# A fused decoder layer: the risk branch outside the batch loop, steering before the last places, and the experts' gate and up product turned

## The chip, the cores and the metric

One Trainium2 chip, one core. The metric is device time of one execution in microseconds (us), here the median of three executions. The engines are TensorE (PE; its weight loads are PEld), VectorE (DVE), ScalarE (ACT), GpSimd (POOL) and SyncE (SP), which only issues transfers.

## What is computed

A decoder layer in fp32 on x of shape (4, 512, 256), with three residual parts, each on a layer norm of x:

```
x = x + self_attention(norm(x))          # causal, 16 heads of 64, bias by distance
x = x + cross_attention(norm(x), ctx)    # 16 heads of 16, 1601 keys a batch, RMS norm of q and k
x = x + experts(norm(x))                 # 32 experts and 8 "zero" experts, top 6 of 40 a token
scores = softmax(h @ classifier.T); top 6 of scores + bias; weight = 2.5 * score
y_e = (silu(h @ Wgate_e.T) * (h @ Wup_e.T)) @ Wdown_e.T      # intermediate width 128
out = h * (sum of weights of zero experts) + sum_e weight_e * y_e
```

## The kernel before, in words

The program has three parts in one block; each engine runs its part of all three one after the other, without a barrier.

**Self attention** (`self_attention`) is not touched.

**Cross attention** (`cross_attention`). A batch is 52 slots (4 groups of 4 heads by 13 tiles of keys). In slot s of batch b PE computes the scores of four heads for one tile of keys (`scores`, line 1226), the product with V of two slots earlier (`times_v`, line 1241), and one step of a written plan (`prepare`): a step of the next batch's keys and queries, or "o" (turning finished heads). ACT takes the exponential of the scores (line 1385, two a slot) and is the engine that must keep pace. The step's result is evacuated by ACT or DVE in slot order. Before each batch PE waits for the steps that prepared it (`prepared[b]`) and branches on the register `risk` (lines 1291 to 1297): one version of the batch subtracts maxima first, the other, the one taken with these inputs, doesn't. In batches 2 and 3 the free slots carry the routing of rows of batches 0 to 2, by the table `ROUTE` (line 670): "rx" turns normalised rows, "rl" is the classification (line 1169), "rk" the ranking of tokens within experts (line 1177). On DVE `pick`, `choose` and `pack` follow; `ROUTE_EXP_AT` says in which slot ACT's exponential and DVE's `choose` stand. DVE also copies the finished heads (`o`, line 1658) in slots 1, 14, 27 and 40 and PE's steps wait for that copy. From batch 3 on POOL scatters the rows of the three routed batches into the tensor `rows` by 72 indirect transfers (`send`), in slot order with its additions to x (line 1063).

**Experts** (`experts`). The last batch is routed when cross attention has ended: DVE normalises, PE classifies, DVE picks six experts (mask), PE ranks and counts. Then DVE works out the places (lines 2120 to 2135), which POOL's 24 row sends wait for (`row_ready`); then the counts (2137 to 2143: each count compared with 16 multiples of 128 and the hits added), prefix sums over 32 experts in five steps of a copy and an addition (2144 to 2150), and the steering (2152 to 2181): for each of 128 tiles where its rows lie and which expert it has. `steer_ready` releases SP, which loads the tiles' rows into a ring of six (line 1885), with a register load of the address for each. The first 40 tiles (`EARLY`) hold only rows of batches 0 to 2; before tile 40 SP waits for the 24 sends of the last batch.

For tile t PE turns its rows (`turn_rows`, line 1986, two tiles ahead), ACT copies them out of PSUM (line 2050), PE multiplies them with gate and up weights, which it streams from `w_all` at an address held in a register (`front`, line 1995), ACT takes silu (2062), DVE multiplies (`gate`, 2207), PE turns the product (`turn_hidden`, 2004), ACT copies it (2068), PE multiplies with the down weights (`back`, 2010), DVE weighs the rows (`weigh`, 2214) and POOL scatters them (`send_tile`, 1937), in a ring of 16 `y` tiles. `owned` (2194 to 2200) finds which of a row's six entries belongs to the tile. POOL does 12 row sends alone and 12 alternating with tile scatters. At the end the scattered rows come back in 16 loads and are summed.

The parts around the change in the code:

## Time and profile before

| | |
|---|---|
| median of 3 executions | 1368.5 us (1365.23 to 1370.36) |
| the profiled execution, its own time | 1370.4 us |
| its span, first to last instruction | 1368.7 us |
| mean granted clock of TensorE | 0.962 of full |
| PE, PEld, DVE, ACT, POOL busy (share of span) | 90%, 53%, 56%, 61%, 51% |

A timeline line gives start, duration, engine, line, operation, destination<-sources, shapes and count, and in brackets the idle time before it with what ended it ("issue": nothing that the profile shows). Line numbers are those of the kernel before. The granted clock is 1.00 at 2.4 GHz and 0.50 at 1.2 GHz.

### The profile page before, as it was taken

The page shows a single profiled execution, that of the slowest core. Times are in us where ns is not written, and L with a number is a line of the kernel's source. Part 1 is how long each engine was busy: PE and PEld are TensorE (multiplying, and loading weights), DVE is VectorE, ACT ScalarE, POOL GpSimd, SP SyncE. Part 2 cuts the span into 40 slices and gives each one's busy share as a digit, 9 for nine tenths or more (in the row PEclk, how much of TensorE's full clock was granted, in tenths as well). Part 3 has the DMA queues.
Part 4 walks back from the last instruction along what each step waited for, and adds up shares of the span by engine and source line. Part 5 has one row for each costly group of instructions (what it writes and reads, how often), then busy time and mean ns, then how long its engine had stood idle before and what let it go on. Part 6 is the DMA issues. An engine that isn't in the chain of part 4 may idle for free.

```text
span 1368.7 us, 26985 instructions
## 1 busy us (share of the span) xinstructions
PE 1226.5 (90%) x8240; PEld 731.5 (53%) x8240; DVE 767.5 (56%) x2628; ACT 828.3 (61%) x1691; POOL 698.5 (51%) x777
## 2 busy tenths in 40 slices
PE   6999999999999875999899989999899359999965
PEld 4666776776676554433243324333232248888854
DVE  6675566557555557362136213624562568888857
ACT  5656456546555335679966996798899235555520
POOL 1776567557557403356036603652477267655640
PEclk9999999999999997999999999999999679999987
DMA  7986566556445521000011001010383746655549
GB/s 240 337 253 228 174 223 232 201 196 222 157 156 188 165 64 47 17 26 24 2 40 34 24 2 47 3 34 1 114 294 120 278 145 195 180 169 166 171 146 383
DMA packets 146277, 195.10 MB, mean 143 GB/s; under 512 B 12592, under 2 KB 133056, under 8 KB 145488
## 3 DMA queue, kind: packets, MB, share of 16 engines
q1 hardware_dynamic: 135376, 162.97, 36.3%
q0 software_dynamic: 10752, 30.26, 6.7%
q8 instruction: 79, 1.29, 0.4%
q14 instruction: 70, 0.57, 0.1%
HBM read 71.01 MB, written 122.18 MB: 141 GB/s over the span
## 4 chain that ended last, share of the span: by engine, by line
PE 66%; ACT 12%; DVE 8%; issue 7%; POOL 3%; DMA 3%; SPq 0%; POOLq 0%; DVEq 0%; ACTq 0%
PE sa_pf L347 11%; ACT xa_probs L1385 9%; PE mo_banks L1995 8%; PE xa_banks L1226 7%; PE xa_banks L1241 5%; PE sa_po L422 5%; PE sa_ps L396 5%; PE xa_banks L1109 5%; PE sa_ptr L407 5%; PE sa_pf L380 4%; PE mo_banks L2010 4%; PE mo_banks L1986 2%; DMA mo_w_all<-parts 2%; PE mo_banks L2004 1%; ACT xa_q_aug L1331 1%
## 5 line engine op out<-in xcount | busy, mean ns | idle before, releaser
L1385 ACT ACTIVATE xa_probs<-xa_banks 128x1024 f32<-128x1024 f32 (+1 forms) x416 | 402.1, 1045 | 94.7 <-PE xa_banks L1226 93.9
L334 POOL TENSOR_SCALAR sa_probs<-sa_probs,sa_recip 128x128 f32<-128x128 f32 (+3 forms) x256 | 274.9, 1087 | 176.2 <-DVE sa_recip L585 176.0
L465 ACT ACTIVATE sa_probs<-sa_probs,sa_neg_max 128x128 f32<-128x128 f32 (+3 forms) x256 | 141.9, 555 | 148.0 <-DVE sa_neg_max L522 147.9
L1241 PE MATMUL xa_banks<-xa_probs,xa_v_one 128*17 128x512 f32 (+1 forms) x1664 | 220.4, 602 | 6.9 <-ACT xa_q_aug L1331 4.6
L1226 PE MATMUL xa_banks<-xa_q_aug,xa_k_aug 32*128 32x512 f32 (+1 forms) x1664 | 154.9, 446 | 21.7 <-issue 12.2
L1937 POOL DMA_INDIRECT parts<-mo_y,mo_dest x128 | 122.8, 959 | 78.9 <-DVE mo_dest L2200 64.3
L522 DVE CUSTOM_DVE_ANT_0 sa_probs<-sa_ps,sa_toeplitz 128x128 f32<-128x128 f32 (+3 forms) x256 | 115.5, 488 | 38.9 <-PE sa_ps L396 36.0
L1995 PE MATMUL mo_banks<-mo_w_all,mo_xs_t 128*128 x512 | 133.0, 383 | 0.0
L1226 PEld LDWEIGHTS xa_banks<-xa_q_aug,xa_k_aug 32*128 32x128 f32 (+1 forms) x1664 | 62.1, 181 | 115.7 <-ACT xa_probs L1385 75.5
L582 DVE COPY sa_pt<-sa_ptr 128x128 f32<-128x128 f32 (+3 forms) x128 | 62.8, 490 | 103.9 <-PE sa_ptr L407 103.8
L407 PE MATMUL sa_ptr<-sa_ident,sa_probs 128*128 128x128 f32 x640 | 94.9, 276 | 6.7 <-ACT sa_pt L488 3.5
L1995 PEld LDWEIGHTS mo_banks<-mo_w_all,mo_xs_t 128*128 128x128 f32 x512 | 88.1, 192 | 7.4 <-issue 0.4
L407 PEld LDWEIGHTS sa_ptr<-sa_ident,sa_probs 128*128 128x128 f32 x640 | 75.9, 141 | 30.0 <-issue 11.5
L969 POOL TENSOR_TENSOR xa_k_area<-xa_k_area 128x256 f32<-128x256 f32 (+1 forms) x39 | 23.9, 612 | 130.9 <-DVE xa_k_area L1556 123.4
L1033 POOL DMA_INDIRECT rows<-xa_k_area,xa_place_i x72 | 70.9, 985 | 37.1 <-issue 20.2
L2050 ACT ACTIVATE mo_xs_t<-mo_banks 128x256 f32<-128x256 f32 x128 | 49.2, 384 | 66.3 <-PE mo_banks L1986 64.5
L422 PE MATMUL sa_po<-sa_pt,sa_v 128*64 128x256 f32 (+3 forms) x512 | 85.0, 454 | 1.0 <-issue 1.0
L1556 DVE TENSOR_TENSOR xa_k_area<-xa_banks,xa_bkv 128x256 f32<-128x256 f32 (+1 forms) x52 | 21.9, 424 | 108.8 <-PE xa_banks L1109 108.5
L2010 PE MATMUL mo_banks<-mo_w_all,mo_hidden_t 128*128 x256 | 76.6, 381 | 0.0
L488 ACT ACTIVATE sa_pt<-sa_ptr 128x128 f32<-128x128 f32 (+3 forms) x128 | 55.0, 429 | 32.1 <-PE sa_ptr L407 30.5
L1241 PEld LDWEIGHTS xa_banks<-xa_probs,xa_v_one 128*17 128x17 f32 (+1 forms) x1664 | 28.0, 95 | 85.9 <-issue 54.7
L2062 ACT ACTIVATE mo_silu<-mo_banks 128x128 f32<-128x128 f32 x128 | 35.5, 278 | 62.8 <-PE mo_banks L1995 62.8
(312 smaller groups left out, 2374.4 us busy)
## 6 DMA issues: line engine op xcount, KB each, us to landing
rows<-sa_blank SPq DMA_DIRECT2D x128, 548.0 KB, 3.7
mo_xs<-rows SPq DMA_DIRECT2D x128, 137.0 KB, 2.2
parts<-sa_blank SPq DMA_DIRECT2D x96, 128.0 KB, 3.8
mo_w_all<-parts SPq DMA_DIRECT2D x16, 768.0 KB, 14.5
xa_raw<-in_ctx_t SPq DMA_DIRECT2D x24, 256.0 KB, 2.8
mo_w_all<-in_gate_up_p SPq DMA_DIRECT2D x2, 2816.0 KB, 16.5
sa_toeplitz<-extended_bias SPq DMA_DIRECT2D x8, 512.0 KB, 7.7
mo_w_all<-in_down_p SPq DMA_DIRECT2D x2, 2048.0 KB, 15.7
```

The lines of the kernel that those rows point to most:

```text
L334: pool.tensor_scalar(probs[:, t % SLOTS, 0:w], probs[:, t % SLOTS, 0:w], recip[:, col:col + 1], None, ALU.mult).then_inc(probs_ready, 1)
L347: last = pe.matmul(out, u, v, start=(n == 0), stop=(n == 3 * chunks - 1))
L407: last = pe.transpose(ptr[t % 2][:, k * P:(k + 1) * P], probs[:, t % SLOTS, k * P:(k + 1) * P], ident[:])
L422: last = pe.matmul(po[a * DH:(a + 1) * DH, k * P:T], v_sb[:, k, h * DH:(h + 1) * DH], pt[:, pt_at(h, k, k):pt_at(h, k, TT)], start=(k == 0 ...
L465: act.activation(probs[:, t % SLOTS, 0:w], probs[:, t % SLOTS, 0:w], ACT.Exp, bias=neg_max[:, i:i + 1], scale=-1.0, accum_out=sums[:, i:i ...
L522: dve.tensor_tensor_reduce(out=probs[:, t % SLOTS, 0:w], in0=ps[t % SCORES][:, 0:w], in1=toeplitz[:, h, w - 1::-1], scale=-1.0 / DH, scala ...
L1226: last = pe.matmul(banks[0:m, 2 * ((n + i // 2) % 3) + i % 2, :], keys, q[rows, :], start=(k == 0), stop=(k == len(parts) - 1))
L1241: last = pe.matmul(banks[32 * i:32 * i + XD + 1, 6 + group % 2, :], v_one[b % 2][0:m, c, 4 * g + i, :], probs[0:m, (2 * j + i // 2) % RING ...
L1385: act.activation(probs[0:m, n % RING, :, :], banks[0:m, 2 * (n % 3):2 * (n % 3) + 2, :], ACT.Exp).then_inc(probs_ready, 1)
L1937: pool.indirect_dma_start(out=parts, out_offset=bass.IndirectOffsetOnAxis(ap=dest[:, t:t + 1], axis=0), in_=y[t % Y_RING][:], in_offset=No ...
L1995: last = pe.matmul(banks[:, 2 + t % 2, 0:2 * INTER], xs_t[t % T_RING][:, c, :], w_all[:, bass.ds(e * (KD * 2 * INTER) + c * 2 * INTER, 2 * ...
L2010: pe.matmul(banks[:, 4 + t % 2, 0:D], hidden_t[t % H_RING][:], w_all[:, bass.ds(e * D + DOWN_AT, D)], start=True, stop=True).then_inc(y_ps ...
```

## The change

- The branch on `risk` stands once, outside the loop over batches, with a loop in each arm.
- Classification, exponential and ranking of routed batches 1 and 2 move by one slot, except the ranking of batch 1, which stays in slot 15.
- PE counts before it ranks; DVE computes counts, prefix sums and steering first and the places after `steer_ready`. The number of tiles of an expert comes from a scaled count that is rounded by adding and subtracting 1.5 * 2^23; the prefix sums read from arrays with 16 zeros ahead, with no copy.
- Gate and up: the weights are the loaded operand and the turned rows are streamed, so the product comes out turned and `turn_hidden`, its copy and its buffers go. ACT copies the tile's gate and up weights (128x512) to a ring of three, with a register load for the address.
- `owned` handles two tiles at once; the product of the last batch's own rows with the weights of the zero experts moves behind the tiles; the load of `acc` moves to tile 40.

The diff, cut to its core (left out: tile declarations with their spacing, semaphores, the inside of the block of places, which is the same in both, and at the end the old `owned`, `gate` and `weigh` and the moved product of own rows):

```diff
@@ -669,13 +669,13 @@
     ROUTED = B - 1
     ROUTE = {(B - 2, 42): ("rx", 0, 0), (B - 2, 44): ("rx", 0, 1), (B - 2, 45): ("rl", 0, 0),
              (B - 2, 51): ("rk", 0, 0), (B - 1, 6): ("rx", 1, 0), (B - 1, 7): ("rx", 1, 1),
-             (B - 1, 9): ("rl", 1, 0), (B - 1, 15): ("rk", 1, 0), (B - 1, 22): ("rx", 2, 0),
-             (B - 1, 23): ("rx", 2, 1), (B - 1, 25): ("rl", 2, 0), (B - 1, 31): ("rk", 2, 0)}
+             (B - 1, 10): ("rl", 1, 0), (B - 1, 15): ("rk", 1, 0), (B - 1, 22): ("rx", 2, 0),
+             (B - 1, 23): ("rx", 2, 1), (B - 1, 26): ("rl", 2, 0), (B - 1, 32): ("rk", 2, 0)}
     ROUTE_CONSTS_AT = (B - 2, 36)
     ROUTE_LOADS_AT = (B - 2, 30)
     ROUTE_LOAD_AT = {(B - 2, 30): 0, (B - 2, 32): 1, (B - 1, 16): 2}
     ROUTE_NORM_AT = {(B - 2, 38): 0, (B - 1, 1): 1, (B - 1, 17): 2}
-    ROUTE_EXP_AT = {(B - 2, 48): 0, (B - 1, 11): 1, (B - 1, 27): 2}
+    ROUTE_EXP_AT = {(B - 2, 48): 0, (B - 1, 12): 1, (B - 1, 28): 2}
     ROUTE_STORE_AT = {(B - 1, 5): 0, (B - 1, 20): 1, (B - 1, 36): 2}
     SEND_FROM = 2
     SENDS_IN_16 = 24
@@ -1288,12 +1288,14 @@
             pe.wait_ge(const_ready, 3)
             pe.wait_ge(gain_done, 1)
             risk = pe.value_load(unsafe[0:1, 0:1], min_val=0, max_val=1)
-            for b in range(B):
-                wait_out(pe, prepared[b])
-                with pe.If(risk > 0):
+            with pe.If(risk > 0):
+                for b in range(B):
+                    wait_out(pe, prepared[b])
                     largest(b)
                     run(b, True)
-                with pe.Else():
+            with pe.Else():
+                for b in range(B):
+                    wait_out(pe, prepared[b])
                     run(b, False)
             run(B, False)
...
@@ -1714,9 +1716,12 @@
+    TO_WHOLE = 1.5 * 2 ** 23
+    ZEROS = 16
+    W_RING = 3
@@ -1774,8 +1777,7 @@
-        n_tiles = sb("n_tiles", [P, 2, E_ROUTED])
-        summed = [sb(f"summed{i}", [P, 2, E_ROUTED]) for i in range(2)]
+        padded = [sb(f"padded{i}", [P, 2, ZEROS + E_ROUTED]) for i in range(3)]
@@ -1800,12 +1802,13 @@
-        hidden = [sb(f"hidden{i}", [P, P]) for i in range(2)]
+        gu = [sb(f"gu{i}", [P, KD * 2 * INTER]) for i in range(W_RING)]
-        hit = sb("hit", [P, TOP_K])
-        hits = sb("hits", [P, 2, TOP_K])
+        hit = sb("hit", [P, 2, TOP_K])
+        hits = sb("hits", [P, 2, 2, TOP_K])
+        n_tiles = padded[2][:, :, ZEROS:]
@@ -1871,13 +1873,13 @@
-            sp.dma_start(acc[:], x2.rearrange("b (t p) d -> p (b t) d", p=P)[:, 0:TT * LAST, :]
-                         ).then_inc(acc_in, 16)
+                    sp.dma_start(acc[:], x2.rearrange("b (t p) d -> p (b t) d", p=P)[:, 0:TT * LAST, :]
+                                 ).then_inc(acc_in, 16)
@@ -1965,13 +1966,13 @@
                                      kept.cls[:, c, :], start=(c == 0), stop=(c == KD - 1))
             last.then_inc(lg_psum, 1)
             pe.wait_ge(mask_ready, 1)
+            pe.matmul(banks[:, 7, 0:E_ROUTED], ones_r[:], counted[:, 0, 0:E_ROUTED], start=True, stop=True)
+            pe.matmul(banks[:, 7, E_ROUTED:2 * E_ROUTED], ones_r[:], counted[:, TT, 0:E_ROUTED],
+                      start=True, stop=True).then_inc(count_psum, 1)
             pe.matmul(banks[:, 6, 0:TT * E_ALL], earlier_r[:], mask[:].rearrange("p t e -> p (t e)"),
                       start=True, stop=False)
             pe.matmul(banks[:, 6, 0:TT * E_ALL], ones_r[:], counted[:, 0:TT, :].rearrange("p t e -> p (t e)"),
                       start=False, stop=True).then_inc(rank_psum, 1)
-            pe.matmul(banks[:, 7, 0:E_ROUTED], ones_r[:], counted[:, 0, 0:E_ROUTED], start=True, stop=True)
-            pe.matmul(banks[:, 7, E_ROUTED:2 * E_ROUTED], ones_r[:], counted[:, TT, 0:E_ROUTED],
-                      start=True, stop=True).then_inc(count_psum, 1)
             pe.wait_ge(diag_ready, 1)
             pe.matmul(banks[:, 5, 0:2 * N_TILES], ones[:], diag[:].rearrange("p a t -> p (a t)"),
                       start=True, stop=True).then_inc(diag_psum, 1)
@@ -1987,24 +1988,21 @@
                                         xs[:, t % X_RING, c * P:(c + 1) * P], ident[:])
                 last.then_inc(t_psum, 1)
-            def front(t, e):
+            def front(t):
                 pe.wait_ge(t_out, t + 1)
+                pe.wait_ge(gu_ready, t + 1)
                 if t >= 2:
                     pe.wait_ge(h_ready, t - 1)
-                for c in range(KD):
-                    last = pe.matmul(banks[:, 2 + t % 2, 0:2 * INTER], xs_t[t % T_RING][:, c, :],
-                                     w_all[:, bass.ds(e * (KD * 2 * INTER) + c * 2 * INTER, 2 * INTER)],
-                                     start=(c == 0), stop=(c == KD - 1))
+                for half in range(2):
+                    for c in range(KD):
+                        at = c * 2 * INTER + half * INTER
+                        last = pe.matmul(banks[:, 2 + t % 2, half * P:(half + 1) * P],
+                                         gu[t % W_RING][:, at:at + INTER], xs_t[t % T_RING][:, c, :],
+                                         start=(c == 0), stop=(c == KD - 1))
                 last.then_inc(gu_psum, 1)
-            def turn_hidden(t):
+            def back(t, e):
                 pe.wait_ge(h_ready, t + 1)
-                if t >= 2:
-                    pe.wait_ge(ht_ready, t - 1)
-                pe.transpose(banks[:, 6 + t % 2, 0:P], hidden[t % 2][:], ident[:]).then_inc(ht_psum, 1)
-
-            def back(t, e):
-                pe.wait_ge(ht_ready, t + 1)
                 if t >= 2:
                     pe.wait_ge(y_ready, t - 1)
                 pe.matmul(banks[:, 4 + t % 2, 0:D], hidden_t[t % H_RING][:],
@@ -2020,9 +2018,7 @@
                                                 min_val=0, max_val=E_ROUTED - 1))
                     if t + AHEAD < N_TILES:
                         turn_rows(t + AHEAD)
-                    front(t, chosen[t])
-                if 1 <= t <= N_TILES:
-                    turn_hidden(t - 1)
+                    front(t)
                 if t >= 2:
                     back(t - 2, chosen[t - 2])
@@ -2050,23 +2046,26 @@
                 act.activation(xs_t[t % T_RING][:].rearrange("p c n -> p (c n)"), banks[:, t % 2, 0:KD * P],
                                ACT.Copy).then_inc(t_out, 1)
+            def copy_weights(t):
+                e = act.value_load(steer[0:1, N_TILES + t:N_TILES + t + 1], min_val=0, max_val=E_ROUTED - 1)
+                if t >= W_RING:
+                    act.wait_ge(gu_psum, t - W_RING + 1)
+                act.activation(gu[t % W_RING][:], w_all[:, bass.ds(e * (KD * 2 * INTER), KD * 2 * INTER)], ACT.Copy
+                               ).then_inc(gu_ready, 1)
+
+            act.wait_ge(steer_ready, 1)
+            act.wait_ge(w_in, 16 * 5)
             for t in range(AHEAD):
+                copy_weights(t)
                 copy_rows(t)
-            for t in range(N_TILES + 1):
+            for t in range(N_TILES):
                 if t + AHEAD < N_TILES:
+                    copy_weights(t + AHEAD)
                     copy_rows(t + AHEAD)
-                if t < N_TILES:
-                    act.wait_ge(gu_psum, t + 1)
-                    if t >= 2:
-                        act.wait_ge(h_ready, t - 1)
-                    act.activation(silu[t % 2][:], banks[:, 2 + t % 2, 0:INTER], ACT.Silu
-                                   ).then_inc(silu_ready, 1)
-                if t >= 1:
-                    act.wait_ge(ht_psum, t)
-                    if t > H_RING:
-                        act.wait_ge(y_psum, t - H_RING)
-                    act.activation(hidden_t[(t - 1) % H_RING][:], banks[:, 6 + (t - 1) % 2, 0:P], ACT.Copy
-                                   ).then_inc(ht_ready, 1)
+                act.wait_ge(gu_psum, t + 1)
+                if t >= 2:
+                    act.wait_ge(h_ready, t - 1)
+                act.activation(silu[t % 2][:], banks[:, 2 + t % 2, 0:P], ACT.Silu).then_inc(silu_ready, 1)
         def run_vector(dve):
             chain = Chain(dve, dve_chain)
@@ -2077,6 +2076,8 @@
                       ).then_inc(xn_ready, 1)
             dve.memset(choice[:, :, E_ALL:], HUGE)
+            for i in range(3):
+                dve.memset(padded[i][:, :, 0:ZEROS], 0.0)
             dve.wait_ge(const_ready, 2)
             dve.tensor_copy(counted[:, 0, :], picked[:].bitcast(F32))
             dve.tensor_copy(meta[:, :, 2, :], spare_no[:])
@@ -2117,39 +2118,20 @@
             dve.scalar_tensor_tensor(out=weights[:], in0=mask[:].bitcast(F32), scalar=ROUTE_SCALE, in1=scores[:],
                                      op0=ALU.mult, op1=ALU.mult)
-            dve.wait_ge(rank_psum, 1)
-            ranks = banks[:, 6, 0:TT * E_ALL].rearrange("p (t e) -> p t e", e=E_ALL)
-            chain.then_wait(dve.tensor_tensor(place[:], ranks, region_at[:].unsqueeze(1)
-                                              .to_broadcast([P, TT, E_ALL]), ALU.add))
...
-            dve.tensor_reduce(meta[:, :, 1, :], same[:], AX.X, ALU.add).then_inc(row_ready, 1)
-
             dve.wait_ge(count_psum, 1)
-            dve.tensor_scalar(counts[:, 0, :], banks[:, 7, 0:E_ROUTED], 1.0 - P, None, ALU.add)
-            chain.then_wait(dve.tensor_copy(counts[:, 1, :], banks[:, 7, E_ROUTED:2 * E_ROUTED]))
-            chain.then_wait(dve.tensor_tensor(
-                past[:], counts[:].unsqueeze(3).to_broadcast([P, 2, E_ROUTED, TILES]),
-                full[:].unsqueeze(1).to_broadcast([P, 2, E_ROUTED, TILES]), ALU.is_gt))
-            chain.then_wait(dve.tensor_reduce(n_tiles[:], past[:], AX.X, ALU.add))
-            held = n_tiles
+            dve.tensor_scalar(counts[:, 0, :], banks[:, 7, 0:E_ROUTED], 1.0 / P, 0.5 / P - 0.5, ALU.mult, ALU.add)
+            chain.then_wait(dve.tensor_scalar(counts[:, 1, :], banks[:, 7, E_ROUTED:2 * E_ROUTED], 1.0 / P,
+                                              0.5 - 0.5 / P, ALU.mult, ALU.add))
+            chain.then_wait(dve.tensor_scalar(counts[:], counts[:], TO_WHOLE, None, ALU.add))
+            chain.then_wait(dve.tensor_scalar(n_tiles, counts[:], TO_WHOLE, None, ALU.subtract))
+            held = padded[2]
             for i in range(5):
-                n = 2 ** i
-                dve.tensor_copy(summed[i % 2][:, :, 0:n], held[:, :, 0:n])
-                chain.then_wait(dve.tensor_tensor(summed[i % 2][:, :, n:], held[:, :, n:],
-                                                  held[:, :, 0:E_ROUTED - n], ALU.add))
-                held = summed[i % 2]
-
-            filled, all_tiles = held[:, 0, :], held[:, 1, :]
+                at = ZEROS - 2 ** i
+                chain.then_wait(dve.tensor_tensor(padded[i % 2][:, :, ZEROS:], held[:, :, ZEROS:],
+                                                  held[:, :, at:at + E_ROUTED], ALU.add))
+                held = padded[i % 2]
+
+            filled, all_tiles = held[:, 0, ZEROS:], held[:, 1, ZEROS:]
             chain.then_wait(dve.tensor_scalar(taken[:], filled, float(EARLY), None, ALU.min))
             dve.scalar_tensor_tensor(out=slot_no[:], in0=taken[:, 0:1], scalar=is_late[:], in1=slot_no[:],
                                      op0=ALU.mult, op1=ALU.add)
@@ -2181,47 +2163,66 @@
                               ).then_inc(steer_ready, 1)
             dve.wait_ge(steer_ready, 1)
+            dve.wait_ge(rank_psum, 1)
+            ranks = banks[:, 6, 0:TT * E_ALL].rearrange("p (t e) -> p t e", e=E_ALL)
+            chain.then_wait(dve.tensor_tensor(place[:], ranks, region_at[:].unsqueeze(1)
+                                              .to_broadcast([P, TT, E_ALL]), ALU.add))
...
+            dve.tensor_reduce(meta[:, :, 1, :], same[:], AX.X, ALU.add).then_inc(row_ready, 1)
+
+            def owned(t):
+                i = t % X_RING
+                for n in (t, t + 1):
+                    dve.wait_ge(xs_in[n % X_RING], 16 * (n // X_RING + 1))
+                chain.then_wait(dve.tensor_tensor(hit[:], xs[:, i:i + 2, D:D + TOP_K],
+                                                  row_no[:, t:t + 2].unsqueeze(2).to_broadcast([P, 2, TOP_K]),
+                                                  ALU.is_equal))
+                chain.then_wait(dve.tensor_tensor(
+                    hits[:], xs[:, i:i + 2, D + TOP_K:].rearrange("p t (a k) -> p t a k", k=TOP_K),
+                    hit[:].unsqueeze(2).to_broadcast([P, 2, 2, TOP_K]), ALU.mult))
+                chain.then_wait(dve.tensor_reduce(own[:, t:t + 2, :], hits[:], AX.X, ALU.add))
+                dve.tensor_tensor(dest[:, t:t + 2], own[:, t:t + 2, 1], spare_at[:, t:t + 2], ALU.max
+                                  ).then_inc(own_ready, 2)
+
+            def gate(t):
+                dve.wait_ge(silu_ready, t + 1)
+                if t >= H_RING:
+                    dve.wait_ge(y_psum, t - H_RING + 1)
+                dve.tensor_tensor(hidden_t[t % H_RING][:], banks[:, 2 + t % 2, P:2 * P], silu[t % 2][:], ALU.mult
+                                  ).then_inc(h_ready, 1)
+
+            def weigh(t):
+                dve.wait_ge(y_psum, t + 1)
+                if t >= Y_RING:
+                    tile_landed(dve, t - Y_RING)
+                dve.tensor_scalar(y[t % Y_RING][:], banks[:, 4 + t % 2, 0:D], own[:, t, 0:1], None, ALU.mult
+                                  ).then_inc(y_ready, 1)
+
+            for t in range(N_TILES):
+                if t % 2 == 0:
+                    owned(t)
+                gate(t)
+                if t >= 2:
+                    weigh(t - 2)
+            weigh(N_TILES - 2)
+            weigh(N_TILES - 1)
+
...
```

## Rows read from the trace of the kernel before

**Rows 1.** The page: busy time of each engine (us, share, instructions).
```profile
PE 1226.5 (90%) x8240; PEld 731.5 (53%) x8240; DVE 767.5 (56%) x2628; ACT 828.3 (61%) x1691; POOL 698.5 (51%) x777
```

**Rows 2.** Window: us, busy PE PEld DVE ACT POOL, granted clock, DMA share, GB/s.
```profile
1150.00:1200.00 50.00, 50.00 (x276) 41.95 (x275) 41.55 (x185) 25.43 (x93) 34.43 (x37) 1.00 0.61 184
```

**Rows 3.** Timeline of PE at the four batch starts (start us, duration us, idle before).
```profile
547.80 1.23 PE L1226 MATMUL xa_banks<-xa_q_aug,xa_k_aug 32*128 32x512 f32 x8 [4.62 <-issue]
...
684.08 1.23 PE L1226 MATMUL xa_banks<-xa_q_aug,xa_k_aug 32*128 32x512 f32 x8 [2.40 <-issue]
...
820.58 0.74 PE L1226 MATMUL xa_banks<-xa_q_aug,xa_k_aug 32*128 32x512 f32 x8 [2.05 <-issue]
...
960.05 1.02 PE L1226 MATMUL xa_banks<-xa_q_aug,xa_k_aug 32*128 32x512 f32 x8 [3.18 <-issue]
```

**Rows 4.** Timeline of PE behind two starts; PE's window (granted clock third).
```profile
685.24 1.91 PE L1241 MATMUL xa_banks<-xa_probs,xa_v_one 128*17 128x512 f32 x8
...
821.25 1.05 PE L1241 MATMUL xa_banks<-xa_probs,xa_v_one 128*17 128x512 f32 x8
...
685.00:687.00 2.00, 2.00 (x12) 0.50 0.00 0
```

**Rows 5.** Timeline of DVE, ACT and POOL in the last batch of the cross attention.
```profile
965.02 0.69 DVE L1658 COPY xa_o<-xa_banks 128x512 f32<-128x512 f32 x1 [1.82 <-PE xa_banks L1241]
...
969.65 1.39 DVE L99 TENSOR_SCALAR xa_k_area<-xa_qb,xa_mean_var,xa_rstd 128x256 f32<-128x256 f32 x4
...
974.52 0.66 PE L1160 MATMUL xa_banks<-xa_ident,xa_k_area 128*128 128x128 f32 x4
...
993.57 0.68 DVE L1658 COPY xa_o<-xa_banks 128x512 f32<-128x512 f32 x1
...
1028.88 22.29 ACT L1385 ACTIVATE xa_probs<-xa_banks 128x1024 f32<-128x1024 f32 x24 [0.20 <-PE xa_banks L1226]
...
1069.88 0.72 POOL L1063 TENSOR_TENSOR xa_x<-xa_x,xa_o_norm 128x256 f32<-128x256 f32 x1 [0.30 <-DVE xa_o_norm L1588]
```

**Rows 6.** Timeline of DVE in the routing of the last batch.
```profile
1088.89 0.33 DVE L2122 TENSOR_TENSOR mo_place<-mo_banks,mo_region_at 128x160 f32<-128x160 f32 x1 [0.57 <-PE mo_banks L1970]
...
1093.90 0.18 DVE L2138 TENSOR_SCALAR mo_counts<-mo_banks 128x32 f32<-128x32 f32 x1
...
1098.33 0.18 DVE L2153 TENSOR_SCALAR mo_taken<-mo_summed 128x32 f32<-128x32 f32 x1
...
1104.04 0.19 DVE L2184 TENSOR_REDUCE mo_zero_w<-mo_weights 128x4 f32<-128x32 f32 x1
```

**Rows 7.** Timeline at the start of the expert tiles: PE.
```profile
1107.55 0.66 PE L1986 MATMUL mo_banks<-mo_ident,mo_xs 128*128 128x128 f32 x2 [4.26 <-DMA mo_xs<-rows]
...
1111.67 1.92 PE L1995 MATMUL mo_banks<-mo_w_all,mo_xs_t 128*128 x4
```

**Rows 8.** Timeline of PE, one tile of the steady stretch.
```profile
1200.07 0.38 PE L1986 MATMUL mo_banks<-mo_ident,mo_xs 128*128 128x128 f32 x2
...
1200.29 1.03 PE L1995 MATMUL mo_banks<-mo_w_all,mo_xs_t 128*128 x4
...
1201.15 0.27 PE L2004 MATMUL mo_banks<-mo_ident,mo_hidden 128*128 128x128 f32 x1
...
1201.70 0.38 PE L1986 MATMUL mo_banks<-mo_ident,mo_xs 128*128 128x128 f32 x2
```

**Rows 9.** Lines by form: weight loads of the classification, 128 columns (x, busy us, mean ns).
```profile
L1169 PEld LDWEIGHTS xa_banks<-xa_k_area,xa_xt 128*128 128x128 f32 x48 | 5.6, 191 | 2.6 <-issue 2.6
```

**Rows 10.** Lines of ACT by form (count, busy us, mean ns).
```profile
L1358 ACT ACTIVATE xa_ct_hi<-xa_raw 128x512 fp32r<-128x512 f32 x4 | 2.5, 622 | 0.0
...
L2062 ACT ACTIVATE mo_silu<-mo_banks 128x128 f32<-128x128 f32 x128 | 35.5, 278 | 62.8 <-PE mo_banks L1995 62.8
```

**Rows 11.** Register load on PE's queue (ns min/median/max), and one scatter on POOL.
```profile
L2019 PEldq TENSOR_LOAD <-mo_steer x128: 295/301/526, 1109.4 to 1318.0; - x128
...
1166.32 0.96 POOL L1937 DMA_INDIRECT parts<-mo_y,mo_dest  x1 [0.30 <-issue]
```

52 lines of the change are left out of this document (18 added, 34 removed).

## The prediction

> **What bounds the kernel now.** I read the page first: PE is busy for 1226.5 of the span's 1368.7 us [rows 1]. A share over stages with different limits says little, so the windows by stage come next, then the timeline of the stages that the change touches. Three places matter.
>
> The cross attention (545 to 1070 us) has four batches. At the start of each, PE stands still for 4.62, 2.40, 2.05 and 3.18 us with "issue" as the only releaser [rows 3]: no engine is late. What is special there in the code is the branch on `risk`, which jumps over the unused version of the batch. After the second start the granted clock is 0.50, the 1.2 GHz level, and after the fourth it is low too: eight matmuls of line 1241 take 1.91 us, against 1.05 us after the third, where the clock stayed at 2.4 GHz [rows 4].
>
> The routing of the last batch (1070 to 1104 us) is a chain on DVE in which PE is nearly idle. Ranks are there at 1088.89, the work on places ends as the counts begin at 1093.90, the prefix sums end at 1098.33, steering is out at 1104.04 [rows 6].
>
> The 128 expert tiles (1111.67 to about 1320 us): in 1150 to 1200 PE is busy for 50.00 of 50 us at full clock, DVE for 41.6, ACT for 25.4, POOL for 34.4 [rows 2]. One tile takes 1.63 us on PE, start to start: two transposes 0.22, gate and up 0.86, the transpose of hidden 0.11, down 0.44 [rows 8]. So PE alone sets that stretch.
>
> **The change, part by part.** Each is counted against the profiled execution (1370.4 us, of which the span is 1368.7), which lies 1.9 above the median of 1368.5; I subtract from 1370.4 and then take off that 1.9.
>
> The branch out of the loop. Four jumps become one. The first stays (4.62). At batch 1 PE stands for 2.40 us, of which it would wait some 0.2 for ACT in any slot: 2.2 to gain. Half clock costs 1.23 - 0.74 at line 1226 and 1.91 - 1.05 at 1241: 1.35 more [rows 3, 4]. Batch 2 gives 2.05. Batch 3 gives 3.18, and about 0.95 of clock. Sum 9.7 us. If the jump were not the cause, it is 0.
>
> What is late next in batch 3. PE arrives 4.1 us sooner, but DVE does not: its copy `o` at 965.02 had idled only 1.82 before it, so the normalising that ends at 971.04 ends at 969.2 at best. The transposes for routing (974.52) would be due 4.1 us sooner, at 970.4 or, without the gaps between the first slots, near 968.7; before them come the end of normalising and the `o_norm` behind it, some 0.8 us more, near 970.0. I take 1.3 us given back [rows 5]. Moving the classification from slot 9 to 10 and the exponential from 11 to 12 moves the 6 us of `choose` behind by a slot of 1.86 us (24 exponentials, two a slot, in 22.29 us); the `o` copy queued after it (993.57) and with it the ranking in slot 15, which is not moved, come later: 1.5 given back, bounds 0 and 1.86. In slots 26, 28 and 32 all three moved together: 0. POOL, whose 72 sends run almost without a gap, ends them 0.3 us before its last add at 1069.88, so POOL's queue is a second bound; it waited 0.30 there [rows 5], and it moves by the 1.85 that its first additions gain. So batch 3 gives 1.3 to 1.85. Cross attention: 3.5 + 2.05 + 1.6 = 7.2, bounds 4 and 10.
>
> Steering first. The 5.0 us from 1088.89 to 1093.90 move behind the steering [rows 6]. Counting and prefix sums, 4.43 us, become four operations and five additions; at 0.22 to 0.24 us each, as the small ones beside them in that chain, about 2.0: 2.4 to gain. Steering comes 7.5 us sooner. What waits for the places instead: the 24 row sends on POOL start some 7.5 us later. They are due before tile 40; with 12 alone and 12 paired with a tile's scatter at 1.27 us each [rows 11] they take 46 us from about 7.4 us after steering, so they end 53 us after steering. Tile 40's load is asked for when tile 34 has been transposed, about 57 us after steering: covered, by 4. DVE's first product of a tile is needed some 8 us after steering; the places take 5: covered too. The ring of 16 y tiles is the nearest thing: tile 11 leaves POOL about when tile 27 is weighed, 0 to 1 us of waiting.
>
> Between steering and the first gate matmul lie 7.6 us, 4.1 of them from the first tile's arrival to the third's [rows 7]. The sends that load the queues in that window in the kernel before are not there at first, and neither is the load of `acc`, which now sits at tile 40 in SP's queue, behind a wait that I found met, with six tiles' lead over PE: cost 0. I take 1.5 us, bounds 0 and 2.5. Start of the tiles: 9.0 us sooner, bounds 7.5 and 10.
>
> The tiles. The transpose of hidden goes: -0.11 us on PE. Gate and up become 8 loads of 128 columns with 128 streamed, in place of 4 loads with 256 streamed. The streaming is the same (0.86). The question is the loads. The nearest row is the classification, which loads the same 128 columns of fp32 and streams only 40, so that streaming hides nothing: 48 loads in three bursts of 16 are busy for 5.6 us, 1.87 a burst; less the last one's own 191 ns, over 15, a load starts every 112 ns [rows 9]. 8 x 0.112 = 0.90, or +0.04. The tile becomes 1.63 - 0.11 + 0.04 = 1.56. Bounds: 1.52 if a load hides fully under 107 ns of streaming, 1.62 if each step has 7 ns more than the row. Over 126 tiles: 8.8 us to gain, from 14 down to 1. I take 112, the only row with short streams behind full loads. The Trainium skill, "TensorE: Matmul & The Clock Gate", section "LDWEIGHTS (loading the stationary operand)", puts a load at its columns over 1.2, 107 ns for 128; by that the tile would be at 1.52. Row 9's 112 decides my sum, and the page's case is the first rival.
>
> ACT loses the copy of hidden and gains one of 128x512, 622 ns in its nearest form. It is busy for 25.43 us over 30.7 tiles, 0.83 a tile [rows 2]; less 0.25 (the silu of the same size takes 278 ns) and with the 0.62 that is 1.2 us [rows 10]. In front of it stands a register load, 301 ns on PE's queue [rows 11]; with the register work behind it I take 0.75. Sequencer and engine overlap in PE's queue, which never pauses for it; so ACT stays below 1.56 and costs 0. DVE: four small operations for two tiles instead of one, about -0.35 us a tile, off the path. The sum of own rows moved behind the tiles (1.9 us) lies in the wait for the gathered parts: 0. At the end one hop less: 0.5.
>
> Sum: 7.2 + 9.0 + 8.8 + 0.5 = 25.5; 1370.4 - 25.5 - 1.9 = 1343. Own range: 4 + 7.5 + 1 + 0.5 = 13 to 10 + 10 + 14 + 0.5 = 34.5, that is 1334 to 1355.5.
>
> **The rivals.** (a) Loads hide fully, as a mechanism: each load runs wholly beside the stream before it, and the stream alone sets the pace; tile 1.52. For it: with 256 streamed the four loads cost nothing [rows 8]. Against: 112 where nothing hides it [rows 9]. 126 x 0.04 = 5 more: 1338. Chance 0.22.
>
> (b) The pauses stay, because "issue" is something else at a batch's start, or DVE and POOL eat them: cross attention gives 0 to 1. For it: the rows name no releaser, so the jump is read from the code; and POOL's last add waited only 0.30, so its queue is nearly as long as PE's path [rows 5]. 1343 + 6.5 = 1349.5. Chance 0.12.
>
> (c) Slower: ACT becomes the bound of the tiles. If ACT's register load starts only when its earlier work has drained, a tile costs 1.2 + about 0.75 = 1.95 us [rows 2, 10, 11]. It decides above 1.56. 0.39 x 126 = 49 us: about 1392. For it: no row shows ACT with a register load; against: PE and SP overlap it. Chance 0.06.
>
> (d) Slower too: a load and a stream of the same rows of the array don't overlap once they are equally short: a pass at 0.107 + 0.112, gate and up at 1.75, 0.85 over my 0.90, 107 us, 1450. Rows 8 speak against it. Chance 0.02. The Trainium skill, same page, "Part 3: Packing small matmuls — row/col tiling", says that a load overlaps a running matmul only when their row groups differ; by that rule this would be the case, and the four loads at no cost in the kernel before disagree with it.
>
> (e) Small waits (the ring of y, tile 40, the ranking) and passes of 120 ns or more together take most of the gain: tiles no shorter, cross attention 3, start 4, so 1361, with a tail to 1372. Chance 0.07.
>
> **How the numbers follow.** Forecast 0.51, (a) 0.22, (b) 0.12, (c) 0.06, (d) 0.02, (e) 0.07. The time is the forecast's, 1343. From 1332 to 1357 the range holds the forecast, (a) and (b), short of their tails. 0.5%, 6.8 us, is about what a measurement of this kernel tells from no change: faster by more than that 0.88 (forecast, (a), (b) and under half of (e)), within it 0.04, slower 0.08 ((c) and (d)).
>
> **What would show it.** Right: PE's idle at batch starts falls from 12.2 us in four to one near 4.6; the place work stands behind steering, which is out some 15 us sooner in the span; no row of line 2004; loads of `gu` 112 ns apart and tiles 1.56 apart. Wrong: loads 107 apart (a); pauses of 2 to 3 us left with "issue" (b); ACT with no idle in 1150 to 1200 and PE waiting for `gu_ready` or `silu` (c); a pass of over 200 ns (d); POOL or `y_sent` before PE near tiles 24 to 40 (e).

## The result and the profile after

The changed kernel takes 1351.16 us (median of 4 runs, 1349.71 to 1354.2), the one before 1369.43 beside it: ratio 0.9866, 95% interval 0.9839 to 0.9893, 18.3 us less. Medians and ratios are over the fast executions alone; four slow ones (1499 to 2281 us) among the variants below are left out. The forecast was 25.5 us less, 1343; the measured time is inside the range.

The spans differ by 19.8 us, 1368.7 to 1348.9. Three marks split them: DVE's last layer norm (it opens the routing of the last batch), the first gate and up matmul, and the last one.

| stretch | before | after | difference | forecast |
|---|---|---|---|---|
| start to the last layer norm | 1070.63 | 1061.03 | -9.6 | -7.2 |
| to the first gate matmul | 41.04 | 32.10 | -8.9 | -9.0 |
| to the last gate matmul | 207.15 | 204.08 | -3.1 | -8.8 |
| to the end of the span | 49.88 | 51.69 | +1.8 | -0.5 |

The page of the changed kernel, busy time (beside [rows 1]):

```profile
PE 1215.9 (90%) x8624; PEld 742.4 (55%) x8624; DVE 717.0 (53%) x2370; ACT 866.5 (64%) x1691; POOL 695.7 (52%) x775
```

PE's waits from 540 to 1000 us (us in total, times, longest), the rows that answer to [rows 3]:

```profile
PE xa_banks L1226 <- issue: 3.3, 1, 3.3
PE xa_banks L1177 <- DVE xa_o L1660: 2.4, 1, 2.4
```

Four pauses with "issue" are one. The second row is new: the ranking of batch 1 in slot 15 waits for DVE's copy of the finished heads, `o`.

The routing and the first tiles, timeline of DVE and PE (beside [rows 6, 7]; line 2162 is the last of the steering, line 2168 the first of the places, line 1999 the first gate matmul):

```profile
1061.03 1.41 DVE L91 BATCH_NORM_STATS2 mo_stats<-xa_x 128x6 f32<-128x256 f32 x4 [0.90 <-POOL xa_x L1063]
...
1079.95 1.26 DVE L2130 TENSOR_TENSOR mo_padded<-mo_padded 128x64 f32<-128x64 f32 x5
...
1086.59 0.33 DVE L2162 TENSOR_SCALAR mo_row_no<-mo_banks,mo_tile_no 128x128 f32<-128x128 f32 x1
...
1086.95 0.33 DVE L2168 TENSOR_TENSOR mo_place<-mo_banks,mo_region_at 128x160 f32<-128x160 f32 x1
...
1093.13 1.28 PE L1999 MATMUL mo_banks<-mo_xs_t,mo_gu 128*128 128x128 f32 x5
```

And where the missing gain is: PE's timeline near tile 40, then SP's, then two windows (us, busy PE PEld DVE ACT POOL, clock, DMA share, GB/s):

```profile
1149.22 1.06 PE L1999 MATMUL mo_banks<-mo_xs_t,mo_gu 128*128 128x128 f32 x8
...
1150.77 1.06 PE L1999 MATMUL mo_banks<-mo_xs_t,mo_gu 128*128 128x128 f32 x8
...
1152.32 1.06 PE L1999 MATMUL mo_banks<-mo_xs_t,mo_gu 128*128 128x128 f32 x8
...
1157.49 0.44 PE L1987 MATMUL mo_banks<-mo_ident,mo_xs 128*128 128x128 f32 x2 [3.68 <-DMA mo_xs<-rows]
1157.76 1.06 PE L1999 MATMUL mo_banks<-mo_xs_t,mo_gu 128*128 128x128 f32 x8
...
1159.83 1.91 PE L1999 MATMUL mo_banks<-mo_xs_t,mo_gu 128*128 128x128 f32 x8
...
1162.51 1.06 PE L1999 MATMUL mo_banks<-mo_xs_t,mo_gu 128*128 128x128 f32 x8
```

```profile
1148.60 0.44 SPq L1881 DMA_DIRECT2D mo_acc<-x  x1
1149.95 16.10 SPq L1887 DMA_DIRECT2D mo_xs<-rows  x8
```

```profile
1150.00:1160.00 10.00, 6.32 (x44) 5.43 (x43) 3.95 (x16) 4.71 (x13) 7.56 (x9) 0.94 1.00 350
...
1200.00:1250.00 50.00, 50.00 (x391) 46.77 (x391) 31.95 (x132) 36.07 (x98) 31.07 (x33) 1.00 0.60 177
```

A steady tile takes 1.545 us (1149.22, 1150.77, 1152.32). At 1148.60 SP issues the 1536 KB load of `acc`. The next row load, issued 1.35 us behind it, lands after 7.5; the DMA engines are at 1.00, and PE stands for 3.68 us. Then one gate and up takes 1.91 us, the 1.2 GHz level. From 1152.32 to 1162.51 three tiles take 10.19 us in place of 4.64: 5.6 us lost.

The same trace shows how short the lead of the row loads is. Tile 40 takes the ring slot of tile 34. The text on the kernel before leaves out that SP waits for two semaphores ahead of such a load: PE has turned the old rows, and DVE's `owned` has read them too. PE turns the rows of tile 34 at 1144.37; `owned` ends its pair, 34 and 35, with line 2194 at 1148.98:

```profile
1144.37 0.38 PE L1987 MATMUL mo_banks<-mo_ident,mo_xs 128*128 128x128 f32 x2
...
1148.98 0.16 DVE L2194 TENSOR_TENSOR mo_dest<-mo_own,mo_spare_at 128x2 int32<-128x2 f32 x1
```

The load of tile 40 goes out at 1149.95, and PE runs out of work at 1153.81 (1157.49 less 3.68): 3.9 us of lead, where six tiles would be 9.3. At this tile it was 4.4 us in the kernel before, in which `owned` did one tile at a time. SP's waits in the whole span, changed kernel, then the kernel before:

```profile
SPq L1885 <- DVE mo_dest L2194: 41.2, 56, 6.2
```

```profile
SPq L1883 <- DVE mo_dest L2200: 52.2, 109, 2.4
```

### The profile page after: what moved, and what is told of

It reads as the page before. It is cut to its first block, busy times and chain, and to the rows that moved or that the text cites. A ratio compares the mean times of both kernels' runs of the same rounds, so it can differ in the third digit from the quotient of the medians.

```text
span 1348.9 us, 27626 instructions
## 1 busy us (share of the span) xinstructions
PE 1215.9 (90%) x8624; PEld 742.4 (55%) x8624; DVE 717.0 (53%) x2370; ACT 866.5 (64%) x1691; POOL 695.7 (52%) x775
## 4 chain that ended last, share of the span: by engine, by line
PE 56%; ACT 14%; issue 11%; DVE 8%; DMA 4%; POOL 3%; ACTq 2%; SPq 1%; POOLq 0%; DVEq 0%
PE sa_pf L347 11%; ACT xa_probs L1387 8%; PE xa_banks L1226 7%; PE xa_banks L1241 6%; PE sa_po L422 5%; PE sa_ps L396 5%; PE xa_banks L1109 5%; PE sa_ptr L407 5%; PE sa_pf L380 4%; PE mo_banks L1999 3%; DMA mo_w_all<-parts 2%; ACT mo_xs_t L2046 2%; ACTq L2050 1%; DMA mo_xs<-rows 1%; PE mo_banks L2008 1%
## 5 line engine op out<-in xcount | busy, mean ns | idle before, releaser
L1999 PE MATMUL mo_banks<-mo_xs_t,mo_gu 128*128 128x128 f32 x1024 | 137.8, 278 | 0.0
L1999 PEld LDWEIGHTS mo_banks<-mo_xs_t,mo_gu 128*128 128x128 f32 x1024 | 127.2, 195 | 0.1
L2053 ACT ACTIVATE mo_gu<-mo_w_all 128x512 f32 x128 | 80.7, 630 | 66.8 <-issue 52.7
L407 PEld LDWEIGHTS sa_ptr<-sa_ident,sa_probs 128*128 128x128 f32 x640 | 75.7, 141 | 30.0 <-issue 11.5
L2201 DVE TENSOR_TENSOR mo_hidden_t<-mo_banks,mo_silu 128x128 f32<-128x128 f32 x128 | 37.4, 292 | 70.7 <-ACT mo_silu L2068 65.9
```

What stands on the lines that cost most here:

```text
L407: last = pe.transpose(ptr[t % 2][:, k * P:(k + 1) * P], probs[:, t % SLOTS, k * P:(k + 1) * P], ident[:])
L1999: last = pe.matmul(banks[:, 2 + t % 2, half * P:(half + 1) * P], gu[t % W_RING][:, at:at + INTER], xs_t[t % T_RING][:, c, :], start=(c == ...
```

## The experiments

All are timed against the kernel before on their own chip. The first four ran on one chip, the next four on another, the last four on a third. Within a set medians compare directly, between sets only the ratios do. One profile can't carry 1 us in the first stretch: in the seven profiles of the first two sets and the result that have the hoist (the branch moved out of the loop) and the new slots, the last layer norm starts from 1058.82 to 1061.73. Most of that is there before any of the removed jumps: the last scores of batch 0 start from 675.04 to 677.85 in these seven, at 676.11 in `loop_branch`, which has all four jumps, and at 680.02 in the kernel before.

**1. Where the load of `acc` stands.** The yardstick, `after_again`:

> The changed kernel itself, as the yardstick of this set: 1351 us, ratio to before 0.987. In its profile PE waits about 3.7 us for the rows of tile 40 to 42, behind the 1536 KB load of acc, and three fronts after it take 1.7 to 1.9 us at the 1.2 GHz level.

Measured 1351.62 us, 0.9863 (0.9842 to 0.9884).

`acc_early`:

```diff
             kept.stored(sp)
+            sp.dma_start(acc[:], x2.rearrange("b (t p) d -> p (b t) d", p=P)[:, 0:TT * LAST, :]
+                         ).then_inc(acc_in, 16)
...
                 if t == EARLY:
                     sp.wait_ge(sent[1], 16 * TT * TOP_K)
-                    sp.dma_start(acc[:], x2.rearrange("b (t p) d -> p (b t) d", p=P)[:, 0:TT * LAST, :]
-                                 ).then_inc(acc_in, 16)
```

> The load of acc goes back to its old place, ahead of the wait for the rows' sends. Theory (the 1536 KB load stands ahead of the row loads in the one queue, and PE starves and then loses its clock): the idle of 3.7 us and the slow fronts go, 7 to 7.5 us less, 1344 us. Rival (the load costs the same wherever it stands, because it takes the DMA engines from the tail of the down-weight loads or from the first row loads): 1350 to 1352 us, with the first front some us later than 1093. Rival (the stretch around tile 40 stalls for another reason, the wait for the last sends): the idle at tile 40 stays, 1351 us.

Measured 1344.26 us, 0.9809 (0.979 to 0.9829): 7.4 less than the yardstick on the same chip (3 to 11 by the two intervals). Timeline of SP, and windows of this variant:

```profile
1061.04 0.63 SPq L1876 DMA_DIRECT2D mo_acc<-x  x1
1086.64 8.58 SPq L1887 DMA_DIRECT2D mo_xs<-rows  x8
```

```profile
1150.00:1160.00 10.00, 10.00 (x79) 9.30 (x78) 6.39 (x27) 7.55 (x21) 7.56 (x9) 1.00 0.66 195
1160.00:1170.00 10.00, 10.00 (x81) 9.40 (x80) 6.35 (x26) 7.18 (x19) 7.56 (x9) 1.00 0.67 204
```

The load now goes out 25.6 us before the first row load and takes 23.0, beside the weights, when nobody needs the queue. PE is busy for 20 of 20 us at full clock. The gates take 198.69 us from first to last, where the result's profile and the yardstick's, with the load at tile 40, show 204.08 and 202.37; the first gate comes 32.23 us after the layer norm, as before the move. So the first theory holds, and the load costs nothing at its old place. Of the 7.4 us the traces show 3.7 to 5.4 in the tiles; the rest is within what two medians can tell.

`acc_act`, the same load by ACT's queue, issued at 1151.1, 2.5 us later than SP did:

```diff
...
+                if t == EARLY - 4:
+                    act.dma_start(acc[:], x2.rearrange("b (t p) d -> p (b t) d", p=P)[:, 0:TT * LAST, :]
+                                  ).then_inc(acc_in, 16)
                 act.wait_ge(gu_psum, t + 1)
```

> The load of acc is issued at the same stretch, but by ACT, so that it stands in no queue ahead of the row loads. Theory A (order in SP's queue is the cause): row loads then take at most 3 to 4 us instead of 7.5, PE's idle there falls under 1 us and the clock stays: 5 to 7 us less, 1345 us. Theory B (the DMA engines' bandwidth is the cause: 1536 KB take about 4.5 us of all 16 engines at 350 GB/s, whoever issues them): the row loads take 6 to 7 us all the same, no gain, 1350 to 1352 us.

Measured 1348.82 us, 0.9838 (0.9821 to 0.9856): 2.8 less than the yardstick, 4.6 more than `acc_early`. PE's timeline:

```profile
1156.17 0.44 PE L1985 MATMUL mo_banks<-mo_ident,mo_xs 128*128 128x128 f32 x2 [0.80 <-DMA mo_xs<-rows]
...
1160.26 0.44 PE L1985 MATMUL mo_banks<-mo_ident,mo_xs 128*128 128x128 f32 x2 [2.33 <-DMA mo_xs<-rows]
```

The 2.8 us are not clear of the two intervals, which overlap; the trace tells more, and it fits neither theory alone. With the queue free, PE still stands for 3.13 us, and its row loads now take up to 7.2. The window 1150 to 1160 has the DMA engines at 0.90, so the bytes taking them from the row loads would fit; no run separates that from other causes. What goes is the fall of the clock behind the pauses: both windows there show 1.00. The two slow tiles lose 3.6 us, where the three in the result and in `after_again` lose 5.6 and 6.1: more than half of the loss is not the order in SP's queue.

`owned_single`: DVE's work on own rows for one tile at a time, as in the kernel before.

> DVE works out own and dest for one tile at a time again, as in the kernel before, so that a slot of the ring of rows is handed back every tile and not in pairs; the load of acc stays at tile 40. If the pairs shorten the lead of the row loads (SP waits for own_ready 41 us in 56 waits in the changed kernel), the idle of 3.7 us at tile 40 falls by 1 to 1.5 us, and the small idles of 0.63 and 0.38 us go; it may save all 7 us if the clock stays up: 1344 to 1349 us. Rival: DVE has 4 more instructions every two tiles, about 0.25 us more a tile beside 1.545 us, and does not bound: 1351 us, with no gain either if the lead isn't what is short.

Measured 1350.41 us, 0.9856 (0.9836 to 0.9875), 1.2 less: no difference. PE's waits for rows rose from 10.7 to 11.6 us in the profile, and the three slow tiles lose 9.2 us. The pairs are not the cause. In the five profiles with this load in SP's queue at tile 40 (these three, `loop_branch` and `places_first`) the loss is 5.6 to 9.3 us, so a difference of up to 3.7 in it can't be put down to an edit.

**2. Each part of the change.** `hoist_alone`: the kernel before, with `with pe.If(risk > 0)` outside `for b in range(B)` and nothing else.

> The kernel before with one edit: the choice between the two branches stands outside the loop over the batches on PE. Theory: the three later pauses of 2.05 to 3.2 us go and little is given back in batch 3: 7 to 9.6 us less, 1361 to 1364 us, ratio about 0.994, with PE's idle at batch starts at 1 pause of about 3.3 to 4.6 us. Rival (the idle goes elsewhere, the rx wait of DVE in batch 3 and the POOL queue give half back): 4 us less, 1367 us. Rival (no gain alone: the later slots are what brought it): 1371 us.

Measured 1359.23 us, 0.9929 (0.991 to 0.9948): 10.1 less. PE's pauses with "issue" at line 1226 fall from 12.2 us in four to 3.7 in two. PE's way through the cross attention, start times and how much sooner than before:

| | before | `hoist_alone` | changed kernel |
|---|---|---|---|
| last scores of batch 0 | 680.02 | 676.06 (4.0) | 677.22 (2.8) |
| scores in slot 12 of batch 3 | 986.46 | 972.61 (13.9) | 973.73 (12.7) |
| scores in slot 19 of batch 3 | 1000.75 | 986.91 (13.8) | 991.19 (9.6) |
| DVE's last layer norm | 1070.63 | 1059.09 (11.5) | 1061.03 (9.6) |

The three removed jumps lie between the first two rows: they give 9.9 us in either kernel. Between slots 12 and 19 the changed kernel gives back 3.2, this one nothing. PE's timeline there, this one, then the changed kernel, then a window of the latter:

```profile
980.62 0.31 PE L1177 MATMUL xa_banks<-xa_ct_hi 128*128 128x160 f32 x1 [0.54 <-issue]
```

```profile
983.55 0.31 PE L1177 MATMUL xa_banks<-xa_ct_hi 128*128 128x160 f32 x1 [2.38 <-DVE xa_o L1660]
...
986.36 1.23 PE L1226 MATMUL xa_banks<-xa_q_aug,xa_k_aug 32*128 32x512 f32 x8
```

```profile
985.00:987.00 2.00, 2.00 (x16) 0.51 (x8) 1.93 (x5) 1.61 (x2) 1.47 (x2) 0.50 0.97 248
```

With the later slots the ranking waits 2.38 us for the copy of `o`, and most of the two slots behind it runs at the 1.2 GHz level. With the old ones PE comes through, but its lead does not reach the layer norm whole: the chain of work goes through POOL's last row sends, at 1056.08 and 1057.34, to its last add at 1058.33, and 2.3 us of the 13.8 are lost there. So the layer norm gains 7.6 from the hoist alone and 6.8 with the slots moved, each counted from the last scores of batch 0; 0.8 in one profile of each is too little to call.

`loop_branch`: the changed kernel with the loop as before.

> The changed kernel with the choice of branch back inside the loop over batches, the slots as changed. If the hoist is the whole of the gain in the cross attention: 8 to 10 us more, 1360 us, ratio to before about 0.993. If the two later slots of the routing brought part of it: less than 8 more. If they cost something that the hoist had to pay for (the ranking waits 2.4 us for the copy of o in the changed kernel): over 10 more.

Measured 1363.69 us, 0.9964 (0.9949 to 0.998). Its ratio lies 1.0% above the yardstick's, some 14 us (10 to 17 by the intervals). The four pauses are back (11.8 us in four), and its layer norm comes at 1072.40, 11.9 later than the yardstick's. PE gives back the 3.2 us between slots 12 and 19 here too, so they are the slots' and not the hoist's. Its stall at tile 40 is also larger: first to last gate takes 208.52 us against 202.37, and this part of the 14 is not the branch's.

`places_first`: the places and their matmuls ahead of the steering again, the rounding kept.

> The changed kernel with the last batch's places worked out ahead of the steering again, on PE and DVE; the rounding stays. Steering is out 5.0 us later, so the first gate matmul comes 5.0 to 6.5 us later (the second number if the row sends of POOL load the queues in that window again), and tile 40's stall may be a little smaller or the same: 1356 to 1358 us. Rival (the order is worth nothing, since PE then waits for something else, the row loads' chain or the weights): 1351 to 1352 us. The remaining 2.4 us of the 7.5 are then the rounding's.

Measured 1356.96 us, 0.9906 (0.9887 to 0.9926), some 6 us over the yardstick's ratio. DVE's timeline, this variant, then the kernel with the hoist alone, which counts by comparisons:

```profile
1059.67 1.40 DVE L91 BATCH_NORM_STATS2 mo_stats<-xa_x 128x6 f32<-128x256 f32 x4 [0.90 <-POOL xa_x L1063]
...
1090.34 0.33 DVE L2179 TENSOR_SCALAR mo_row_no<-mo_banks,mo_tile_no 128x128 f32<-128x128 f32 x1
```

```profile
1059.09 1.41 DVE L91 BATCH_NORM_STATS2 mo_stats<-xa_x 128x6 f32<-128x256 f32 x4 [3.26 <-POOL xa_x L1063]
...
1092.13 0.33 DVE L2182 TENSOR_SCALAR mo_row_no<-mo_banks,mo_tile_no 128x128 f32<-128x128 f32 x1
```

Layer norm to steering is 33.04 us with comparisons and places first, 30.67 with rounding, 25.56 with both edits (1061.03 to 1086.59). So rounding is worth 2.4 us and the order 5.1, one profile of each.

`old_tiles`: `acc_early` with the gate, up, hidden and copies of the kernel before.

```diff
...
-                        last = pe.matmul(banks[:, 2 + t % 2, half * P:(half + 1) * P],
-                                         gu[t % W_RING][:, at:at + INTER], xs_t[t % T_RING][:, c, :],
+                    last = pe.matmul(banks[:, 2 + t % 2, 0:2 * INTER], xs_t[t % T_RING][:, c, :],
+                                     w_all[:, bass.ds(e * (KD * 2 * INTER) + c * 2 * INTER, 2 * INTER)],
...
+                if 1 <= t <= N_TILES:
+                    turn_hidden(t - 1)
```

> The variant with the load of acc at its old place (1344.3 us), with the old form of the tiles: 4 gate and up passes of 256 columns read straight from the weights, hidden turned on PE and copied by ACT, no copy of the weights. Tile 1.63 in place of 1.545 us: 126 x 0.085 = 10.7 us more, 1355 us. Rival (the tiles' pace is set by the queue of row loads or POOL and the turned form won little): 1346 to 1349 us. PE is then busy all the time with passes of 214 ns, at full clock.

Measured 1350.92 us, 0.9873 (0.9852 to 0.9894). `acc_early` ran on the other chip; the ratio is 0.64% above its, some 9 us (5 to 13 by the intervals). Timelines of PE, `acc_early` and `old_tiles`:

```profile
1200.36 1.06 PE L1999 MATMUL mo_banks<-mo_xs_t,mo_gu 128*128 128x128 f32 x8
...
1201.90 1.06 PE L1999 MATMUL mo_banks<-mo_xs_t,mo_gu 128*128 128x128 f32 x8
```

```profile
1199.80 1.03 PE L1997 MATMUL mo_banks<-mo_w_all,mo_xs_t 128*128 x4
...
1201.42 1.03 PE L1997 MATMUL mo_banks<-mo_w_all,mo_xs_t 128*128 x4
```

The pace is 1.545 against 1.63 us. From first to last gate it is 198.69 against 207.73 us, 9.0 us for the new form, near the 8.8 forecast. The end takes 1.4 of it back: last gate to end of span is 51.5 against 50.1 us, most of it in the two long waits for the gathered parts (12.65 and 16.59 us against 12.40 and 15.79). Why those loads are longer stays open.

**3. The last set.** `old_slots` is the changed kernel with the routing slots of the kernel before. `acc_split` loads `acc` in 12 pieces of 128 KB from tile 60 on. `early_slots` is `acc_early` with the old slots. `early_slots_ring8` has `X_RING = 8` besides.

> The changed kernel with the classification, exponential and third ranking of the routing in the slots of the kernel before (9, 11, 25, 27, 31). Theory (the later slots push the copy of o and leave PE's ranking waiting 2.38 us in slot 15): that wait goes, and 1 to 2 us of the end, 1349.5 to 1350.5 us, with the last layer norm of DVE 1 us nearer to 1059. Rival (the slots were moved because DVE is late in batch 3 after the hoist, and going back brings a wait of PE for mo logits or for exp): 1352 to 1354 us.

> The load of acc in 12 pieces of 128 KB, one ahead of every fifth row load from tile 60 on, all in the one queue. If it is the one large load at the head of the queue that starves PE: each piece costs about 0.7 us of queue, well inside the lead, and nothing is lost, 1344 to 1346 us. If any load beside the rows and scatters costs its bytes (1536 KB at 350 GB/s are 4.4 us): 1348 to 1349 us. The idle at tile 40 would stay if the wait for the sends were its cause: it should be under 1 us.

> The load of acc at its old place and the slots of the kernel before. If both effects add: 1342 to 1343.5 us, ratio about 0.980. If the slots do nothing: 1344.3 us, as with the load alone (0.9809).

> As the one before with a ring of 8 slots for gathered rows in place of 6, so two more row loads are asked for ahead. In the variant with the load moved, PE still waits 2 to 3 us for row loads of 4 to 5 us beyond the first. If the lead is what is short: 1 to 2 us less than the one before, 1341 to 1342 us. If the waits are all at the start, where no lead can help: no difference.

| kernel | median us | ratio | interval |
|---|---|---|---|
| before | 1471.75 | | |
| `old_slots` | 1481.84 | 1.0067 | 1.0038 to 1.0097 |
| `acc_split` | 1473.78 | 1.0016 | 0.9997 to 1.0035 |
| `early_slots` | 1475.41 | 1.0022 | 1.0 to 1.0045 |
| `early_slots_ring8` | 1476.39 | 1.0026 | 1.0005 to 1.0047 |

On this chip the kernel before itself takes some 100 us more than on the other two, so every expected time missed, and none of the four beats it. Inside the set one thing can be read: the load of `acc` at its old place (the only difference of `early_slots` from `old_slots`) is worth 6.4 us, near the 7.4. `acc_split` differs from `early_slots` in the slots and in when the pieces go out, and takes the same time, with no wait for rows above 1.2 us behind 1175; that the pieces cost nothing fits and is not shown apart. With the longer ring PE's waits for rows fall from 11.4 to 5.1 us and the time does not, but here rows are not what PE waits for most. What the slots cost can't be read from these times, since the changed kernel did not run here; the table under `hoist_alone` shows it.

Up to 940 us PE's busy time in `early_slots` is that of `acc_early` within 3 us, its granted clock within 0.02. Then, while the sends of rows and the weight loads run, its chain shows pauses that the other chips don't have, and later SP's steps of 0.7 us, which are 0.04 to 0.34 in `acc_early` (chain of work, start us, us, what):

```profile
984.91 6.71 another core or an unknown queue
...
991.66 2.86 another core or an unknown queue
...
1310.03 0.71 SPq L1885
...
1311.52 0.70 SPq L1886
1312.26 0.72 SPq L1887
1312.99 1.18 DMA mo_xs<-rows
```

The layer norm comes at 1125.54, the gates take 263.7 us from first to last in place of 198.7, and yet an undisturbed gate and up still takes 0.89 us. From 1160 to 1420 PE's longest waits are for DVE's product (22.8 us), DVE's for ACT's silu (74.4), and ACT stands 36 us with a releaser that the profile doesn't know. A shorter path on PE is worth little there. The cause stays open. Slower loading of instructions is not what the profile shows: on its page the busier instruction queue has 76 packets and 0.4%, as in `acc_early`.

## Why the prediction was right, and which step failed

**The failed step** is the sentence that `acc` "now sits at tile 40 in SP's queue, behind a wait that I found met, with six tiles' lead over PE: cost 0". It cost 7.4 us by the medians and 5.6 in the first profile. Two things in it were wrong. The lead was never six tiles: a slot comes free with DVE's `owned`, not with PE's turning, so the row load of tile 40 went out 3.9 us before PE wanted it. The trace of the kernel before had this to read, in SP's 52.2 us of waits for `mo_dest`. And the load's own time was not set against the lead: it takes 8.0 us to landing, and the row load behind it 7.5. The wait for the sends was met, as said: POOL is done with the last row send at 1136.3. The sentence also took the load out of the window before the first tile as a gain. There it had landed: issued at the layer norm, 23 us to landing, 2.6 us before the first row load in `acc_early`.

**The time alone decides little.** 1351.2 is nearer to rival (b), 1349.5, than to the forecast of 1343, and the range held both; that (b) is false comes from the traces and `hoist_alone`. With the load of `acc` at its old place the change gives 26.8 us, near the 25.5, in which errors of both signs meet, as follows.

**Branch.** 7.2 forecast, 9.6 in the traces. But 2.8 of these are there before the second batch, ahead of every removed jump: 1.3 is the first pause, which was to stay at 4.62 and is 3.31 (3.1 to 3.8 in all eight profiles with the hoist, 4.3 in `loop_branch`, so it may be the hoist's), and the rest is what profiles differ by. Counted from there the layer norm gains 6.8, in the seven profiles 6.5 to 7.5. The terms: the three jumps with their clock 9.9, where 9.7 was said; given back 3.2, where 2.8 was said. In that give-back the wait for the normalised rows, 1.3, did not come, and the ranking's, 1.5, came as 3.2 with its half clock, above its bound of 1.86. So the sum is right, and partly by luck. The bound by POOL's queue was named and is real: in `hoist_alone` it holds 2.3 us back. That run's median is 10.1 less, its layer norm 7.6 sooner by this count; the interval of the ratio reaches down to 7.

**Steering.** 7.5 forecast, 7.5 measured (33.04 to 25.56), split as said: 5.0 and 2.4 (which make 7.4) against 5.1 and 2.4. From steering to the first gate, forecast 1.5 less, is 8.0 us before and 6.5 after. It is 6.5 to 6.7 in five more profiles with steering first and 7.9 in `after_again`, against 7.8 and 9.4 in `places_first` and `hoist_alone`: borne out, with one exception. The load of `acc` has no part in it, `acc_early` shows 6.7.

**Tiles.** The pace is 1.545 us where 1.56 was said. Eight passes take 0.89, and their loads start 110 to 112 ns apart, as in [rows 9]; the streams alone started every 108 ns for 128 columns in the kernel before. So the loads are not fully hidden, and rival (a), 1.52, is false. The pace alone would give 10.7 us; small waits for rows take some 2 of it, so the 9.0 of `old_tiles` meets the forecast of 8.8 partly by luck. The Trainium skill gives 107 ns for such a load ("TensorE: Matmul & The Clock Gate", "LDWEIGHTS (loading the stationary operand)"); by the trace it is 4 ns more. In "Part 3: Packing small matmuls — row/col tiling" of the same page ("TensorE: Matmul & The Clock Gate") the Trainium skill lists overlap of a load with a running matmul only between different row groups, though its text above the list also names a background weight buffer. Here eight loads for the same rows overlapped their streams, or a pass would have been the 0.22 us of rival (d).

**ACT** did not become the bound (c). In the window 1200 to 1250 by line:

```profile
L2053 ACT ACTIVATE mo_gu<-mo_w_all 128x512 f32 x33 | 20.8, 630 | 14.3 <-issue 14.3
```

It stands for 0.43 us a tile behind the register load, less than the 0.75 I allowed, and has 36.1 us of work in 50. Rival (b), that the pauses stay, fell with `hoist_alone`. Rival (e) held in two of its parts, the stall at tile 40 and the ranking. The end was 1.8 us longer and not 0.5 shorter; why stays open.

## What to carry to other kernels

Ahead of moving a large load, write down what it displaces: its own time to landing, and the lead of the small loads behind it in microseconds, not in tiles. Take the lead from the trace, from a load's issue to the use of its data, and name the wait that really frees the slot: a ring of six gave 3.9 us of lead here, two and a half tiles. Put it where the queue is idle anyway; at its old place here the same change gives 26.8 us (1371.05 to 1344.26) in place of 19.4. Line two profiles up at a point ahead of the change before a difference behind it is put down to the change. Time a gain on more than one chip before it is believed in full.
